# Layer 1's local scores in 32-row column tiles of PE, each with its own band of keys

## What is computed

```
x = _layernorm(x + _L0_attn_ref(x, ...))      # causal attention, rope, 16 heads of 16
x = _layernorm(x + _L0_ffn_ref(x, ...))       # top-1 of 8 experts per token
x = _layernorm(x + _L1_attn_ref(x, ...))      # local attention (below) mixed by a gate with a latent one
x = _layernorm(x + _L1_ffn_ref(x, ...))       # top-1 of 8 experts per batch
# the local attention of layer 1, window w = 128:
dist = q_pos[:, :, None] - k_gpos[:, None, :]
allowed = (dist > 0) & (dist <= w) & (k_gpos[:, None, :] >= 0)
scores = jnp.where(allowed, einsum(q, k) * scale, NEG)
attn = jax.nn.softmax(scores, axis=-1);  out = attn @ v
```

## Time and profile before

| | us |
|---|---|
| median of 3 runs | 1584.42 (1584.26 to 1594.23) |
| the profiled execution, its time | 1600.77 |
| its span (first to last instruction) | 1599.0 |
| PE busy | 1333.7 (83%) |
| DVE busy | 952.3 (60%) |
| ACT busy | 609.2 (38%) |
| POOL busy | 277.4 (17%) |

### The profile page before, as it was taken

How to read it: one execution, slowest core, us unless ns; L and a number is a source line. 1 busy time by engine, 2 the same in 40 slices (tenths; PEclk the granted TensorE clock), 3 DMA queues, 4 the chain that set the end, 5 groups by cost and what they waited for, 6 DMA issues and landing times. The chain is left out here.

```text
span 1599.0 us, 25207 instructions
## 1 busy us (share of the span) xinstructions
PE 1333.7 (83%) x8819; PEld 831.2 (52%) x8819; DVE 952.3 (60%) x2373; ACT 609.2 (38%) x1152; POOL 277.4 (17%) x294
## 2 busy tenths in 40 slices
PE   4488888888888889739995699899989898989864
PEld 1234444444544455439995455656555555555532
DVE  3365666665666657227777365666666767676642
ACT  0034444444443445315552134344344344434331
POOL 2111120212111200111112121021222222212022
PEclk9799999999999999859998689999999999999975
DMA  3432614141414132524211424404040404040000
GB/s 109 121 102 68 164 55 115 61 100 61 100 61 100 48 90 83 170 76 163 70 61 40 130 73 106 100 21 126 21 116 31 116 32 117 31 104 1 15 14 13
DMA packets 68235, 127.40 MB, mean 80 GB/s; under 512 B 8320, under 2 KB 58128, under 8 KB 64656
## 3 DMA queue, kind: packets, MB, share of 16 engines
q1 hardware_dynamic: 65040, 117.39, 26.8%
q0 software_dynamic: 3072, 8.41, 1.7%
...
## 5 line engine op out<-in xcount | busy, mean ns | idle before, releaser
L533 DVE TENSOR_REDUCE first_maxima<-bank 128x1 f32<-128x512 f32 (+3 forms) x352 | 220.4, 638 | 212.9 <-PE bank L346 209.7
L482 ACT ACTIVATE arena<-pair 128x512 f32<-128x512 f32 x320 | 187.2, 596 | 318.1 <-PE pair L375 315.6
L1308 ACT ACTIVATE second_probs<-pair 128x512 f32<-128x512 f32 (+1 forms) x256 | 137.5, 541 | 300.1 <-PE pair L1173 292.0
L1458 DVE TENSOR_REDUCE second_maxima<-bank 128x2 f32<-128x512 f32 (+1 forms) x224 | 153.8, 688 | 143.5 <-PE bank L1149 141.9
L343 PE MATMUL bank<-stacks 96*128 96x256 bf16 (+3 forms) x512 | 126.8, 304 | 46.6 <-DVE first_maxima L533 25.0
L324 PE MATMUL bank<-first_xT,w_qkv 128*128 128x512 f32 x256 | 135.6, 660 | 9.7 <-DVE first_halves L518 5.5
L368 PE MATMUL pair<-stacks 99*128 99x512 bf16 (+3 forms) x512 | 124.3, 304 | 17.0 <-DMA stacks<-first_m_turned 14.7
L1147 PE MATMUL bank<-second_k_stack,second_q_stack 96*128 96x256 bf16 (+1 forms) x512 | 90.4, 269 | 7.7 <-DMA second_k_stack<-parked 6.2
L1170 PE MATMUL pair<-second_q_stack,second_k_stack 99*128 99x256 bf16 (+1 forms) x512 | 94.4, 266 | 0.6 <-ACT second_probs L1308 0.6
L1173 PE MATMUL pair<-logits,constants_bf 128*128 128x512 bf16 (+1 forms) x256 | 93.7, 366 | 0.0
L343 PEld LDWEIGHTS bank<-stacks 96*128 96x128 bf16 x512 | 44.3, 98 | 93.4 <-DVE first_maxima L533 45.2
(11 more groups left out here) (324 smaller groups left out, 2417.5 us busy)
## 6 DMA issues: line engine op xcount, KB each, us to landing
...
```

The source lines that it names most:

```text
L482: act.activation(PT[:, s:s + len(heads), lo:lo + each], ex[n % 3][:, 0:len(heads) * each].rearrange("p (h q) -> p h q", h=len(heads)), ACT ...
L533: dve.tensor_reduce(nm[:, i, qt, heads[0]:heads[0] + len(heads)], mx[n % 2][:, 0:wide].rearrange("p (h k) -> p h k", h=len(heads)), AX.X, ...
L1308: act.activation(PT[:, s:s + len(heads), lo:lo + each], ex[n % 2][:, 0:len(heads) * each].rearrange("p (h q) -> p h q", h=len(heads)), ACT ...
L1458: dve.tensor_reduce(nm[:, i, qt, heads[0]:heads[0] + len(heads)], mx[n % 2][:, :].rearrange("p (h k) -> p h k", h=len(heads)), AX.X, ALU.m ...
```

## The change

`MAX` becomes five steps. The 12 pairs of (query tile, head) with tiles 1 to 3 are taken three to a bank, each pair 160 columns wide, and tile 0 keeps its one step of 4 heads x 128. Within a step of three pairs each pair is four matmuls with 32 weight columns (32 queries) and 160 moving columns (the band of keys of those 32 queries), which go to the four groups of 32 partitions of the bank; the mask is four matmuls with 32 weight columns and 3 x 2 x 32 moving columns, since only the two corner triangles of 32 x 32 of a band need one. The `exp` steps keep their contents; each 256-column product becomes four matmuls with 32 weight columns (32 keys) and 160 moving columns (128, 96, 64 and 32 in key tile 3), and the mask four of 128 columns (64 in tile 3). What lies outside the bands in the two `ex` banks is set to the mask once, by one more matmul each, and stays. ACT's exp reads and writes what it did. DVE's reductions read 480 columns in place of 512, and are five per group in place of seven.

Since the times of the five max steps are g - 2 + (u + 0.6) / 5, they stand at other places of the list than the seven did.

```diff
 KROWS = ROWS + 3
+SUB = 32
+BAND = P + SUB
 GH = 4
...
         self.eng.wait_ge(self.sem, self.n)
+def corners(ap, s, count):
+    return ap.rearrange("p (r a c) -> p r a c", r=1, c=SUB)[:, :, s:s + 5:4, :].to_broadcast([P, count, 2, SUB])
...
     WIDTH, SLOTS = 896, 6
-    MAX = [(q, hs) for q in (1, 2, 3) for hs in ([0, 1], [2, 3])] + [(0, [0, 1, 2, 3])]
+    MAX = [(4, 7), (7, 10), (10, 13), (13, 16), (0, 4)]
     EXP = [([0], [0, 1]), ([1], [0, 1]), ([0, 1], [2]), ([0, 1], [3]), ([2], [0, 1]), ([3], [0, 1]), ([2, 3], [2]), ([2, 3], [3])]
...
                             pe.wait_ge(lp["s_max"], n - 1)
-                        qt, heads = plan.MAX[j]
-                        k0 = max(0, qt - 1) * P
-                        wide = (qt + 1) * P - k0
-                        for y, hh in enumerate(heads):
-                            h = i * GH + hh
-                            pe.matmul(mx[n % 2][:, y * wide:(y + 1) * wide], q[0:ROWS, h, qt * P:(qt + 1) * P],
-                                      k[0:ROWS, h, k0:k0 + wide], start=(y == 0), stop=True, skip_group_check=True)
-                        pe.matmul(mx[n % 2][:, :], m["idb"][:, :], spread(mS[:, 2 * P - wide:2 * P], wide, len(heads)),
-                                  start=False, stop=True, skip_group_check=True).then_inc(lp["s_ps"], 1)
+                        first, end = plan.MAX[j]
+                        if first == 0:
+                            for hh in range(GH):
+                                h = i * GH + hh
+                                pe.matmul(mx[n % 2][:, hh * P:(hh + 1) * P], q[0:ROWS, h, 0:P], k[0:ROWS, h, 0:P],
+                                          start=(hh == 0), stop=True, skip_group_check=True)
+                            ins = pe.matmul(mx[n % 2][:, :], m["idb"][:, :], spread(mS[:, P:2 * P], P, GH),
+                                            start=False, stop=True, skip_group_check=True)
+                        else:
+                            for y, u in enumerate(range(first, end)):
+                                qt, h = u // GH, i * GH + u % GH
+                                for s in range(P // SUB):
+                                    q0 = qt * P + s * SUB
+                                    pe.matmul(mx[n % 2][s * SUB:(s + 1) * SUB, y * BAND:(y + 1) * BAND], q[0:ROWS, h, q0:q0 + SUB],
+                                              k[0:ROWS, h, q0 - P:q0 + SUB], start=(y == 0), stop=True, skip_group_check=True)
+                            for s in range(P // SUB):
+                                out = mx[n % 2][s * SUB:(s + 1) * SUB, 0:3 * BAND].rearrange("p (y a c) -> p y a c", a=5, c=SUB)
+                                ins = pe.matmul(out[:, :, 0:5:4, :], m["idb"][:, s * SUB:(s + 1) * SUB], corners(mS, s, 3), start=False, stop=True,
+                                                skip_group_check=True)
+                        ins.then_inc(lp["s_ps"], 1)
                     elif kind == "turn":
...
                         heads, tiles = plan.EXP[j]
-                        lo, width = 0, min(2, NT - tiles[-1]) * P
-                        for hh in heads:
+                        if n < 2:
+                            pe.matmul(ex[n][:, :], m["idb"][:, :], spread(mT, 2 * P, 2), start=True, stop=True, skip_group_check=True)
+                        for y, (hh, kt) in enumerate((hh, kt) for hh in heads for kt in tiles):
                             h = i * GH + hh
-                            for kt in tiles:
-                                pe.matmul(ex[n % 2][:, lo:lo + width], k[0:KROWS, h, kt * P:(kt + 1) * P],
-                                          q[0:KROWS, h, kt * P:kt * P + width], start=(lo == 0), stop=True, skip_group_check=True)
-                                lo += width
-                        pe.matmul(ex[n % 2][:, 0:lo], m["idb"][:, :], spread(mT[:, 0:width], width, lo // width), start=False,
-                                  stop=True, skip_group_check=True).then_inc(lp["c_ps"], 1)
+                            for s in range(P // SUB):
+                                k0 = kt * P + s * SUB
+                                wide, lo = min(BAND, S - k0), 2 * P * y + s * SUB
+                                pe.matmul(ex[n % 2][s * SUB:(s + 1) * SUB, lo:lo + wide], k[0:KROWS, h, k0:k0 + SUB],
+                                          q[0:KROWS, h, k0:k0 + wide], start=(y == 0), stop=True, skip_group_check=True)
+                        for s in range(P // SUB):
+                            out = ex[n % 2][s * SUB:(s + 1) * SUB, :].rearrange("p (y a c) -> p y a c", y=2, c=SUB)
+                            if tiles[-1] == NT - 1:
+                                ins = pe.matmul(out[:, :, s, :], m["idb"][:, s * SUB:(s + 1) * SUB], spread(mT[:, s * SUB:(s + 1) * SUB], SUB, 2), start=False, stop=True,
+                                                skip_group_check=True)
+                            else:
+                                ins = pe.matmul(out[:, :, s:s + 5:4, :], m["idb"][:, s * SUB:(s + 1) * SUB], corners(mT, s, 2), start=False, stop=True,
+                                                skip_group_check=True)
+                        ins.then_inc(lp["c_ps"], 1)
                     elif kind == "values":
...
                         lo, each = plan.AT[tiles[0]], len(tiles) * min(2, NT - tiles[-1]) * P
+                        scores = ex[n % 2][:, :].rearrange("p (h q) -> p h q", h=len(heads))
                         act.wait_ge(lp["c_ps"], n + 1)
...
                         act.activation(PT[:, s:s + len(heads), lo:lo + each],
-                                       ex[n % 2][:, 0:len(heads) * each].rearrange("p (h q) -> p h q", h=len(heads)),
-                                       ACT.Exp, scale=SCALE).then_inc(lp["exps"], 1)
+                                       scores[:, :, 0:each], ACT.Exp, scale=SCALE).then_inc(lp["exps"], 1)
                     elif kind == "o_in":
...
                         dve.wait_ge(lp["s_ps"], n + 1)
-                        qt, heads = plan.MAX[j]
-                        dve.tensor_reduce(nm[:, i, qt, heads[0]:heads[0] + len(heads)],
-                                          mx[n % 2][:, :].rearrange("p (h k) -> p h k", h=len(heads)),
+                        first, end = plan.MAX[j]
+                        wide = P if first == 0 else BAND
+                        dve.tensor_reduce(nm[:, i, :, :].rearrange("p t h -> p (t h)")[:, first:end],
+                                          mx[n % 2][:, 0:(end - first) * wide].rearrange("p (u k) -> p u k", k=wide),
                                           AX.X, ALU.max, negate=True).then_inc(lp["s_max"], 1)
```

## The result

| | before | changed |
|---|---|---|
| median | 1593.36 us of 14 runs (1584.26 to 1606.09) | 1580.30 us of 14 runs (1567.74 to 1590.52) |
| ratio to before | | 0.9919, 95% interval 0.9893 to 0.9945 |
| span of the profiled execution | 1599.0 us | 1579.8 us |
| mean granted clock over that span | 0.925 | 0.896 |

The changed kernel is 0.8% faster: within 1%, where 2.9% was forecast, and outside the range. Of the 41 us between the forecast's 1539 and the measured 1580, 9 come from the base: 14 runs of before have a median of 1593.4, the first three had 1584.4. The other 32 are the size of the gain, 13 us where 45 was forecast. The two profiled executions are 19 us apart, but 5 of these lie ahead of layer 1's first matmul (877.9 us in before, 872.8 in the changed kernel), in code that the change doesn't touch.

The account below looks back on a forecast made before the run. PE was taken as the bound, held at some waits by chains of other engines. 100 - 20 (shapes) - 23 (chains) - 12 (clock) = 45 us less, from 1584.4 to 1539, 2.9% faster; range 1508 to 1570.

Parts of the forecast that it names:

- Part 1, products and masks: PE's max and exp steps in layer 1: shorter by 3.14 us a group, 100 us over 32 groups.
- Rows 6: Trace rows at the values steps: 8 weight loads and 4 matmuls started within 0.052 us, some 13 ns a pair.
- the floor of rows 7: Trace rows of three short matmuls, 23 to 25 ns each; between column tiles, such a floor would make a round 100 ns.
- Part 2, changes of shape: On PE, each tile shape change costs about 0.11 us; 23 more a batch cost 2.5 us, 20 us in all.
- Part 3, DVE: DVE's reductions of 480 columns take 655 ns, five a group; 6 us less a batch, from 53.3 to 47.
- Part 4, the chains: Longer PE waits on chains of other engines take back 2.9 us a batch, 23 in all.
- The new wait at turn_z: Stretch from out to turn_z: about 1.0 us of PE's saving lost to a new wait there.
- that from the second turn_z to rl: Stretch at the first place of the order, 3.96 us before; about 0.7 of PE's saving lost, chain only 0.4 shorter.
- Part 5, the clock: PE's thinner stretches in layer 1 bring one or two more half-clock falls a batch, 12 us in all.
- Chains and clock take all: Rival: of 80 us, chains take 45 and the clock 25, leaving a 10 us gain, 1574; chance 0.10.
- The issue floor: Rival: matmuls start 25 ns apart even in different column tiles; 19 us less, 1565; chance 0.12.
- The tiles that don't overlap: Rival: PE's column tiles run one after another, 69 ns per matmul; 1690 to 1740 us; chance 0.05.

Follow-up runs that it names:

- e5_max_only: The max steps of the change alone (32-column tiles, bands of 160, five reductions) in before, exp steps as before; ratio to before 0.9916.
- e6_exp_only: The exp steps of the change alone in before, max steps and their seven reductions as before; ratio to before 0.9981.
- e3_no_mask: Before without the mask matmuls of layer 1's local scores, which leaves the scores unmasked; ratio to before 0.9867, median 1579.06 us.
- the filled pair: The changed kernel and before, each with the same 29 useless matmuls a batch ahead of PE's waits; ratios to before 0.9679 and 0.9938.
- the moved pair: The changed kernel and before, each with the same four waiting steps moved later in the order; ratios to before 0.9613 and 0.9858.
- e9_moved: The changed kernel with rl, up, the first turn_a and the second turn_x moved later, no work added; ratio to before 0.9613, 1528.88 us.

## Why the prediction was wrong

**What bounds the kernel** was read rightly: PE, with chains that hold it at a few places. But it was read from one batch of before in which the clock never fell. What the clock would do in a thinner batch isn't in such a window.

**Part 1, products and masks: right.** In the changed kernel's timeline around the third place of the order:

```profile
1355.10 0.32 PE L1191 MATMUL pair<-second_q_stack,second_k_stack 99*32 99x160 bf16 x8
1355.25 0.23 PE L1199 MATMUL pair<-logits,constants_bf 128*32 128x128 bf16 x4
1355.31 1.03 PE L1214 MATMUL pair<-second_probs,second_values 128*32 128x256 f32 x16
1356.17 0.38 PE L1162 MATMUL bank<-second_k_stack,second_q_stack 96*32 96x160 bf16 x12
1356.38 0.26 PE L1166 MATMUL bank<-logits,constants_bf 128*32 128x192 bf16 x4
1356.46 0.31 PE L1191 MATMUL pair<-second_q_stack,second_k_stack 99*32 99x160 bf16 x8
```

A max step takes 0.29 us from start to start (1356.17 to 1356.46), as forecast, and an exp step 0.21 (1355.10 to 1355.31), where 0.19 was forecast. Rows 6 were the right ones to go by; the floor of rows 7 doesn't hold between column tiles, since it would have given 0.40 and 0.30. The tiles overlap. The Trainium skill's floor of about 25 ns (TensorE: Matmul & The Clock Gate, Wait — 56ns, not 53.3ns?) is thus no bound here: 16 matmuls in 0.29 us are 18 ns apart.

**Part 2, changes of shape: right in size for one, probably low in sum.** A q and k projection that takes 1.71 us when nothing changes behind it lasts 1.81 from start to start here (1353.29 to 1355.10), where tiles follow: 0.10. Over whole batches, e5_max_only's 21 changes more go with 1.6 us more of rest, 0.08 each, and e6_exp_only's 42 with 5.1, 0.12 each. The 23 more of the change were to take 2.5 us a batch; the rest that isn't idle time grew by 4.0. e3_no_mask has 1.5 us more of such rest with no change of shape more, so shapes can be 2.5 of the 4.0, and what the other 1.5 is wasn't found.

**Part 3, DVE: right.** The reductions of 480 columns take 655 ns, to the nanosecond what was forecast, and DVE is busy 48 us of a batch, where 47 was forecast. In layer 1 by shape, 1000 to 1540:

```profile
L1486 DVE TENSOR_REDUCE second_maxima<-bank 128x3 f32<-128x480 f32 x103 | 67.3, 655 | 95.9 <-PE bank L1166 95.1
```

**Part 4, the chains: too large, and part 2's shortfall hid it.** Shapes and chains were to take 5.4 us a batch and the rest grew by 4.7, but that the sum came near is in part luck: PE's idle time grew by 0.7 us a batch, where longer waits were to take 2.9. The new wait at turn_z is 0.3 us and not 1.0; that at up went from 0.6 to 0.8; and that at v shrank from 1.6 to 0.6, where the prediction held its length for fixed. One stretch went as said: that from the second turn_z to rl lasts 3.89 us where it lasted 3.96, so nearly all of PE's saving there went.

**Part 5, the clock: the step that failed.** "I expect one or two more a batch, 1 to 2 us a batch, and take 12 in all." The mechanism was named and its size missed. Three of the first four batches had 24 us at 0.50, where the forecast had 3.4 or 6.8 more than the 5 of before; their excess is some 10 us each. Over all of layer 1 the excess grew by 36 us in place of 12. It took "twice that if every wait brings one" for the far end, which is still 24. Two things were left out. Four places of a batch, not one or two, were close to a fall: before's trace has falls at three of them now and then (the earlier trace rows is one, near pool), and in three of the first four batches of the changed kernel all four have one. And a fall isn't always one short stretch: behind up it lasted 13.6 us, though PE was busy nearly all of that time. Before's own trace had one of 10.2 us behind up, which the prediction didn't use:

```profile
1152.50:1162.70 10.20, 10.20 (x29) 5.28 (x28) 5.68 (x17) 2.13 (x4) 3.47 (x3) 0.50 0.11 39
```

With the clock at what it measured the sum is 45 + 12 - 36 = 21 us of gain. The 6 us that shapes and chains took beyond their 43 leave 15, and layer 1 shows 14, the medians 13.

**The rivals.** "Chains and clock take all" gave 1574 and came nearest, with a chance of 0.10. Its split was off: it had 45 for the chains beside 20 for shapes, and 25 for the clock, and layer 1 shows 49 for chains and shapes together and 36 for the clock. The issue floor had a gain of 19 us, not far off either, so the time alone doesn't tell them apart; the step lengths above do. The tiles that don't overlap fell by the same rows.

The chances (0.84 for faster by over 1%) hung on the clock as well: with the clock held the change is worth 2.5 to 2.6% of before, which is near the forecast's 2.9%, in the filled pair and the moved pair alike.

What stays open: what exactly PE's clock is decided by. The runs show that filling the idle time around rl and up, or moving the steps that wait, prevents most falls. They also show a batch with the same waits and no fall there, and a kernel (e6_exp_only) with 6.7 us of columns less a batch and no loss of clock in its first four. It was not tried which of the moves in e9_moved brings how much.
